# Context attention with gate and the query, key and value projections as two unrolled stages over four batches

## The reference, cut to what matters

```python
memory_proj = einsum('bme,de->bmd', memory, W_mem)             # memory: (4, 1601, 256)
scores = einsum('bnd,bmd->bnm', hidden, memory_proj) / sqrt(512)
attn = softmax(scores)
memory_context = einsum('bnm,bmd->bnd', attn, memory_proj)
gate = sigmoid(concat([hidden, memory_context]) @ W_gate.T + b_gate)
x = rmsnorm(hidden + gate * memory_context, norm_w)            # the norm of the first layer
...
vm = expert_mask(token_type_ids)                               # by token: v or l expert
y = rmsnorm(x, ln_in_w)
mixed = where(vm, y @ v_qkv, y @ l_qkv)                        # (4, 512, 1536): q, k, v
q, k = rotary(q, k)
```

## Time and profile before

| | |
|---|---|
| median of 3 runs | 2446.51 us (2446.05 to 2450.79) |
| the profiled execution | 2442.05 us, its span 2440.2 us |
| busy share of the span: PE, DVE, ACT, POOL | 86%, 63%, 40%, 19% |
| mean granted clock of TensorE | 0.912 |
| set-up | 0 to 30.0 us |
| four passes of the loop | 30.0 to 805.4 us |
| self-attention | from 805.4 us |

### The profile page before, as it was taken

How to read it: one execution, slowest core, us unless ns; L and a number is a source line. 1 busy time by engine, 2 the same in 40 slices (tenths; PEclk the granted TensorE clock), 3 DMA queues, 4 the chain that set the end, 5 groups by cost and what they waited for, 6 DMA issues and landing times. The chain is left out here.

```text
span 2440.2 us, 33165 instructions
## 1 busy us (share of the span) xinstructions
PE 2094.5 (86%) x12597; PEld 1365.8 (56%) x12614; DVE 1537.2 (63%) x2208; ACT 973.9 (40%) x1707; POOL 473.7 (19%) x483
## 2 busy tenths in 40 slices
PE   5985985986798699958883999999999799999868
PEld 3673664664566355547771344444443578778756
DVE  5176367376458477664446899999993466666444
ACT  1132132222223255525440688888888222221111
POOL 0211211211103011132220022222222122122111
PEclk8987987988898699989995899999999899999979
DMA  4026025224313866345648243445430234334232
GB/s 154 26 80 222 18 74 184 68 61 146 119 44 125 190 149 167 85 151 208 232 175 165 32 82 77 86 88 93 78 77 15 81 92 114 89 105 117 68 92 70
DMA packets 192596, 262.29 MB, mean 107 GB/s; under 512 B 27896, under 2 KB 108924, under 8 KB 190612
## 3 DMA queue, kind: packets, MB, share of 16 engines
q1 hardware_dynamic: 184278, 248.68, 37.7%
q0 software_dynamic: 7856, 10.90, 1.7%
q10 hardware_dynamic: 288, 0.27, 0.0%
HBM read 193.20 MB, written 64.47 MB: 106 GB/s over the span
## 5 line engine op out<-in xcount | busy, mean ns | idle before, releaser
L1638 DVE TENSOR_REDUCE quarters<-ps 128x2 f32<-128x804 f32 x512 | 483.1, 991 | 51.8 <-PE ps L1672 50.4
L1603 ACT ACTIVATE pT_x<-ps 128x512 f32<-128x512 f32 (+1 forms) x832 | 451.6, 595 | 104.1 <-PE ps L1700 76.7
L1672 PE MATMUL ps<-kx_ring,qx_ring 63*128 63x402 f32 x1024 | 234.0, 469 | 41.0 <-DMA kx_ring<-cross_k_by_part 29.1
L1715 PE MATMUL ps<-pT_x,vx_ring 128*17 128x256 f32 (+1 forms) x3328 | 261.5, 387 | 0.2 <-ACT osb_x L1585 0.2
L190 DVE TENSOR_TENSOR w_lo<-w_raw,w_hi 128x512 fp32r<-128x512 f32 (+3 forms) x309 | 244.7, 792 | 10.6
L188 DVE CAST w_hi<-w_raw 128x512 fp32r<-128x512 f32 (+3 forms) x309 | 157.3, 509 | 138.8 <-PE ps L196 94.0
L1672 PEld LDWEIGHTS ps<-kx_ring,qx_ring 63*128 63x128 f32 x1024 | 100.3, 193 | 233.9 <-DVE quarters L1638 123.3
L194 PE MATMUL ps<-mi_h,w_hi 128*128 128x512 f32 (+1 forms) x440 | 175.0, 398 | 37.3 <-issue 26.1
L1700 PE MATMUL ps<-qx_ring,kx_ring 64*128 64x512 f32 (+1 forms) x832 | 175.0, 417 | 6.4 <-ACT pT_x L1603 2.6
L196 PE MATMUL ps<-mi_l,w_hi 128*128 128x512 f32 (+1 forms) x440 | 174.3, 396 | 0.0
L195 PE MATMUL ps<-mi_h,w_lo 128*128 128x512 f32 (+1 forms) x440 | 173.5, 394 | 0.0
(11 more groups left out here) (271 smaller groups left out, 4450.1 us busy)
## 6 DMA issues: line engine op xcount, KB each, us to landing
kx_ring<-cross_k_by_part SPq DMA_DIRECT2D x96, 200.2 KB, 7.4
w_raw<-L_xattn_l_qkv SPq DMA_DIRECT2D x48, 256.0 KB, 2.9
w_raw<-L_xattn_v_qkv SPq DMA_DIRECT2D x48, 256.0 KB, 2.7
q_ring<-self_q_by_part SPq DMA_DIRECT2D x48, 256.0 KB, 4.1
k_ring<-self_k_by_part SPq DMA_DIRECT2D x48, 256.0 KB, 6.5
w_raw<-L_xattn_l_gate SPq DMA_DIRECT2D x40, 256.0 KB, 2.9
w_raw<-L_xattn_l_up SPq DMA_DIRECT2D x40, 256.0 KB, 2.9
w_raw<-L_xattn_l_down SPq DMA_DIRECT2D x40, 256.0 KB, 2.7
```

The source lines that it names most:

```text
L1603: nc.scalar.activation(pT[0:kn, u % 3, j, :], ps[0:kn, 5 + v % 3, :], ACT.Exp, scale=SCALE)\
L1638: nc.vector.tensor_reduce(out=quarters[:, g % 2, pair, :, q, quarter], in_=ps[:, at:at + 2, 0:MAXW], axis=AX.X, op=ALU.max)\
L1672: last = nc.tensor.matmul(ps[:, at + par, 0:MAXW], q_r[rows, g % RING, pair, q * P:(q + 1) * P], k_r[rows, g % RING, pair, k0:k0 + MAXW], ...
L1715: last = nc.tensor.matmul(ps[j * HD:j * HD + CHD + 1, 4, queries], v_r[0:kn, g % RING, kt, j, :], pT[0:kn, u % 3, j, queries], start=kt == ...
```

## The change

The set-up, the loop and its two blocks are replaced by two blocks that go over all batches, written out one batch after another.

`gated_context` does the set-up and, for each batch, the attention to the context and the gate up to `h`, which it stores as `fused_d` (not yet normed). The split memory weight, `w12`, the transposed memory weight and the x half of the gate weight stay in SBUF for all batches. x has two buffers. The loads of the next batch are issued inside the current one. Row maxima are found in halves of two banks each, alternating with `gate_from_x`, which now does one output tile at a time. The scores use two banks instead of three. The projection of the next x stands between the last steps of a batch.

`queries_values_keys` begins with the last batch (its h is still in SBUF), splits all 24 weight tiles once and keeps them, rounding them on ScalarE and subtracting on VectorE. For each batch the order is queries, values, keys (before: queries, keys, values). The four rotations of the keys are done within the first pieces of the next batch. The squares and their sums use four tiles, and the results go to memory piece by piece from small rings. The first norm's row is stored as `norm_d`, and `projections` applies it with the norm weight to the loaded stream.

```diff
+            for n in range(RAW, len(tiles)):
+                load_w(sp, n, tiles[n], wl, s["s_ws"])
+            for b in range(B):
+                if b:
+                    sp.wait_ge(s["s_g"], 2 * DT * b)
+                    sp.dma_start(fused_d[b - 1], h[:, :, :]).then_inc(s["s_up"], 16)
+                if b + 1 < B:
+                    load_x(b + 1)
+                    load_context(b + 1)
+                    load_rows(b + 1)
+            sp.wait_ge(s["s_g"], 2 * DT * B)
+            sp.dma_start(fused_d[B - 1], h[:, :, :]).then_inc(s["s_up"], 16)
+            sp.wait_ge(s["s_up"], 16 * B)
...
+            for b in range(B):
+                for kt, (k0, kn) in enumerate(KEY_TILES):
+                    n = KT * b + kt
+                    act.wait_ge(s["s_sc"], n + 1)
...
+                    nc.scalar.activation(pT[0:kn, n % 3, :], ps[0:kn, other_bank(b, 2 + kt % 2), :], ACT.Exp,
...
+                    if b + 1 < B and 4 <= kt < 4 + DT:
+                        round_x(b + 1, kt - 4)
+                for e in range(ET):
+                    act.wait_ge(s["s_tm"], ET * b + e + 1)
+                    if b:
+                        act.wait_ge(s["s_b"], DT * b)
+                    nc.scalar.activation(cn_h[:, e, :], tmp[:, e, :], ACT.Copy).then_inc(s["s_cnh"], 1)
+                if b + 1 < B:
+                    round_u(b + 1)
+                    round_context(b + 1)
+                for j in range(DT):
+                    act.wait_ge(s["s_c"], DT * b + j + 1)
+                    if b:
...
+                    else:
...
+                    nc.scalar.activation(eg[:, j, :], ps[:, gate_bank(b, j), :], ACT.Sigmoid, bias=cols[:, 4, j:j + 1])\
+                        .then_inc(s["s_eg"], 1)
...
+            pe.wait_ge(s["s_tabc"], 2 + ET)
+            for b in range(B):
+                pe.wait_ge(s["s_uh"], ET * (b + 1))
+                pe.wait_ge(s["s_th"], NB * (b + 1))
+                if b:
+                    pe.wait_ge(s["s_eg"], DT * b)
+                for j in range(DT):
+                    maxima(b, 2 * j)
+                    maxima(b, 2 * j + 1)
+                    gate_from_x(b, j)
+                pe.wait_ge(s["s_mx"], HALVES * (b + 1))
+                pe.wait_ge(s["s_dg"], ST * (b + 1))
+                scores(b, 0)
+                scores(b, 1)
+                for kt in range(KT):
+                    values(b, kt)
+                    if kt + 2 < KT:
+                        scores(b, kt + 2)
+                if b + 1 < B:
+                    project(b + 1, 0)
+                pe.wait_ge(s["s_un"], ET * (b + 1))
+                pe.wait_ge(s["s_acc"], KT * (b + 1))
+                for q in range(ST):
+                    last = nc.tensor.matmul(ps[:, other_bank(b, 0), q:q + 1], acc[:, q * P:(q + 1) * P], ones[:, 0:1],
+                                            start=True, stop=True)
+                last.then_inc(s["s_sum"], 1)
+                if b + 1 < B:
+                    project(b + 1, 1)
+                pe.wait_ge(s["s_rq"], b + 1)
+                for q in range(ST):
+                    last = nc.tensor.matmul(ps[:, other_bank(b, 1), q * P:(q + 1) * P],
+                                            rq[:, q:q + 1].broadcast_to((P, P)), ident[:, :], start=True, stop=True)
+                last.then_inc(s["s_rep"], 1)
+                if b + 1 < B:
+                    project(b + 1, 2)
+                    project(b + 1, 3)
+                for k in range(ET):
+                    pe.wait_ge(s["s_cnl"], ET * b + k + 1)
+                    for j in range(DT):
+                        cut = slice(j * P, (j + 1) * P)
+                        last = three(ps[:, gate_bank(b, j), :], w12h[:, k, cut], w12l[:, k, cut],
+                                     cn_h[:, k, :], cn_l[:, k, :], False, k == ET - 1)
+                        if k == ET - 1:
+                            last.then_inc(s["s_c"], 1)
+                if b == 0:
+                    pe.wait_ge(s["s_ws"], DT + ET)
                 for j in range(DT):
                     cut = slice(j * P, (j + 1) * P)
+                    if j == 2 and b + 1 < B:
+                        pe.wait_ge(s["s_ul"], ET * (b + 2))
+                    for k in range(ET):
+                        last = three(ps[:, other_bank(b, j), :], wth[:, k, cut], wtl[:, k, cut],
+                                     cn_h[:, k, :], cn_l[:, k, :], k == 0, k == ET - 1)
+                    last.then_inc(s["s_b"], 1)
...
+weights, GROUPS, G = [t["L1_xattn_l_qkv"], t["L1_xattn_v_qkv"]], (0, 2, 1), 2 * DT
+NT, NK = 3 * G, 6
+turns = [B - 1] + list(range(B - 1))
...
+            for i in range(B):
+                store_keep(i)
+                if i:
+                    for j in range(DT):
+                        store_piece(2 * DT * (i - 1) + DT + j)
+                if i + 1 < B:
+                    sp.wait_ge(s["s_x"], 2 * DT * (i + 1))
+                    sp.wait_ge(s["s_sq"], 2 * DT * (i + 1))
+                    sp.dma_start(h[:, :, :], fused_d[turns[i + 1]]).then_inc(s["s_hin"], 16)
+                    load_tokens(i + 1)
+                sp.wait_ge(s["s_rs"], 4 * i + 2)
+                sp.dma_start(norm_d[turns[i]:turns[i] + 1, :], rs0[0:1, :]).then_inc(s["s_r0u"], 16)
+                for j in range(DT):
+                    store_piece(2 * DT * i + j)
+                for a in range(ST):
+                    sp.wait_ge(s["s_vn"], ST * i + a + 1)
+                    sp.dma_start(vs_d[turns[i]].rearrange("g p a n -> p a g n")[:, a, :, :],
+                                 v_nat[:, a % 2, :].rearrange("p (g n) -> p g n", n=P)).then_inc(s_uv[a % 2], 16)
...
+                round_x(0, n)
+                round_w(n)
             for n in range(2):
                 for k in range(DT):
+                    square(0, n, k)
+            for n in range(G, 2 * G):
+                round_w(n)
+            for i in range(B):
+                if i:
+                    keep_plain(i - 1, 1)
+                    for j in range(2):
+                        round_piece(2 * DT * (i - 1) + DT + j)
+                root(i, 0)
+                if i:
+                    for j in range(2, DT):
+                        round_piece(2 * DT * (i - 1) + DT + j)
+                root(i, 1)
+                keep_plain(i, 0)
+                if i == 0:
+                    for n in range(2 * G, 3 * G):
+                        round_w(n)
+                for j in range(DT):
+                    round_piece(2 * DT * i + j)
+                keep_values(i)
+                if i + 1 < B:
+                    for n in range(2 * DT):
+                        round_x(i + 1, n)
+                        square(i + 1, n // DT, n % DT)
+            keep_plain(B - 1, 1)
...
+            def sums(i, n):
+                pe.wait_ge(s["s_sum"], 3 * (2 * i + n + 1))
+                if i:
+                    pe.wait_ge(s["s_t2"], 2 * DT * (i - 1) + DT + n + 1)
+                nc.tensor.matmul(ps[:, bank(3 * i + 1, n), :], ones[:, :], sq[:, 2 + n, :], start=True, stop=True)\
+                    .then_inc(s["s_ss"], 1)
+            def run(i, t0):
+                for n in range(3 * G):
+                    project(i, n, t0)
+                    if n < 2 and i:
+                        rotate(i - 1, 1, 2 * n)
+                        rotate(i - 1, 1, 2 * n + 1)
+                    if n == 3:
+                        sums(i, 0)
+                        sums(i, 1)
+                    if G <= n < G + 2:
+                        rotate(i, 0, 2 * (n - G))
+                        rotate(i, 0, 2 * (n - G) + 1)
+                    if n == G + 4:
+                        pe.wait_ge(s["s_t2"], 2 * DT * i + 1)
+                        pe.wait_ge(s["s_tab"], 5 * i + 3)
+                        for a in range(ST):
+                            last = nc.tensor.matmul(ps[:, bank(3 * i, 0), a:a + 1], rs1[0:1, a * P:(a + 1) * P], ones[0:1, 0:1],
+                                                    start=True, stop=True)
+                        last.then_inc(s["s_rc"], 1)
+            for i in range(B):
+                pe.wait_ge(s["s_k"], NK * (i + 1))
+                early = nc.tensor.value_load(early_v[0:1, turns[i]:turns[i] + 1], min_val=0, max_val=1)
+                with nc.tensor.If(early > 0):
+                    run(i, 0)
+                with nc.tensor.If(early < 1):
+                    run(i, S - P)
+            for j in range(DT):
+                rotate(B - 1, 1, j)
...
-                sp.dma_start(streams[b % 2][:, :, :], gated_d[b]).then_inc(s["s_hin"], 16)
+                sp.dma_start(streams[b % 2][:, :, :], fused_d[b]).then_inc(s["s_hin"], 16)
+                if b:
+                    sp.wait_ge(s["s_scl"], DT * b)
+                sp.dma_start(norm_rows[:, :], norm_d[b:b + 1, :].broadcast_to((P, S))).then_inc(s["s_hin"], 16)
...
-                dve.wait_ge(s["s_hin"], 16 * (b + 1))
+                dve.wait_ge(s["s_hin"], 32 * (b + 1))
+                for j in range(DT):
```

(25 more changed lines are left out.)

974 lines of the change are left out of this document (508 added, 466 removed).

## The result

The changed kernel takes 2308.91 us (median of 4 runs, 2307.88 to 2309.82), against 2447.73 us before on the same chips: ratio 0.943, 95% interval 0.9415 to 0.9448. That is 139 us less; 129 to 130 us were forecast, and the forecast time was 2316 us. The profiled execution spans 2308.0 us, against 2440.2, 132 us less.

The account below looks back on a forecast made before the run. TensorE's order of work was taken to bound a pass while it works, nothing useful at the seams. Self-attention's start moves from 805.4 to 674 us, less 2: 129 to 130 us gained, 2312 profiled, 2316 median; range 2272 to 2376.

Parts of the forecast that it names:

- set-up, to the first row maximum: Start of the kernel: constants land at 12 us, then TensorE and ScalarE work; 39 us, range 34 to 45, against 46.7 before.
- context stage: Attention to the context and gate, all batches: 79 us of TensorE work plus 0.9 us hand-overs per batch, stalls covered.
- the seam: Between the two new blocks: last VectorE steps, store, barrier, token load and small steps; TensorE starts again at 378.4 us.
- second stage, first batch: First batch of queries, values and keys: 76.7 us, with 12.9 us waiting and 128-column pieces at the lower clock.
- three more batches: Later batches of queries, values and keys, weights resident: 65.2 us each, 195.6 us together, including 7 us clock loss each.
- tail, to self-attention: After the last keys: four uncovered rotations, VectorE and ScalarE steps in turn, store and barrier; 23 us, ending at 674 us.
- the projections: Stage applying the first norm by four VectorE steps of 0.75 us per batch; only the first batch pays, 2 us.
- The wait for the sums: Second stage, first batch: TensorE stands still from 391 us until GpSimd has added ScalarE's squares, at 403 to 404; 12.9 us.
- I take half of the loss and the return, 3.5 us: Blocks of 48 narrow matmuls, second stage: half of 4.8 us clock loss, about half of 2 us return; 7 us per batch.
- Rival (a): Clock holds in the second stage's narrow blocks: 8 x 3.5 = 28 us less, 2288 us; chance 0.17.
- Rival (b): Second stage bound by the chain ScalarE, GpSimd, VectorE: sharing costs 13.4 us per batch, 54 us, 2370 us; chance 0.21.
- Adding 4.5 us to the sum: Whole kernel: the median of the runs lies 4.5 us above the profiled execution, so 2312 becomes 2316 us.

## Why the prediction was right, and where its terms were off

The sum was right to 2 us for the profiled execution (2312 forecast, 2309.8 measured), and the mechanism is shown by the experiments. But that it came within 2 us is luck, since terms that were off by up to 14 us balance each other:

| step | forecast | measured | off by |
|---|---|---|---|
| set-up, to the first row maximum | 39 | 47.1 | +8.1 |
| context stage | 321.6 | 322.2 | +0.6 |
| the seam | 17.8 | 18.4 | +0.6 |
| second stage, first batch | 76.7 | 77.8 | +1.1 |
| three more batches | 195.6 | 181.8 | -13.8 |
| tail, to self-attention | 23 | 15.8 | -7.2 |
| the projections | +2 | +9.8 | +7.8 |

- **Set-up.** Too short. The step was "I let them land at 12 us, more than twice the 5.4 us of a 1 MB load alone". They landed at 19.7 us. Beside them stood 5.2 MB of loads on the other queue, not the 4 MB of the estimate, and the small ones waited their turn among these. With these held back they landed at 12.9, which is the number that the estimate was good for.
- **Context stage.** Right: 83.3 us for the first batch and 79.3 for the next two, where 83.7 and 79.9 were said. The last took 80.3, not 78.1; by the prediction's own terms it is 79.9 - 5.6 + 4.7 = 79.0, so 78.1 left the hand-overs out. The alternation of maxima and gate (2.7 us), the projection between the last steps (10.3) and the loads a batch ahead (15.2) each showed its worth when undone.
- **Second stage, first batch.** The sum hit, the parts less. The wait for the sums was 6.9 us, not 12.9, since ScalarE began its squares 9.2 us after TensorE's start, where the prediction had VectorE's eight steps end at 12.6, and the additions took 1.26 to 1.47 us instead of 1.54. TensorE's first four pieces and the sums took 22.2 us (26.1 forecast), the narrow block 10.9 (10.2), the values 24.3 (20.3), the keys 20.3 (20.1). In the values' time are the 3.7 us for rs_col, which the prediction didn't have. Nor did it price in this batch what sets the start of the values, the root behind ScalarE's eight roundings of weights: its product ended 0.3 us before the narrow block was through, so that the wait and the half clock that it did price stood beside a chain of the same length.
- **The other three.** The step that failed was "I take half of the loss and the return, 3.5 us". The narrow block of the queries took 5.73 us at clock 1.00, where 48 x 0.214 = 10.3 us is the price at the lower level. What remains over the work of 56.7 us is 2.3 to 2.5 us ahead of each batch, where the branch stands (the profile charges them to a low part of x), and some 2 us of clock. Rival (a), with a chance of 0.17, is what happened in these three batches. Taken alone, its 28 us less would have been too much: the first batch did lose its block, and the other three kept 3 to 4 us each of pause and clock.
- **Sharing between VectorE and GpSimd.** Rival (b) did not decide. The sharing is there: from 465 us on, 16 of VectorE's masks of x took 1205 ns in the mean, against 749 before. A mask took 1.63 to 1.68 us beside an addition of GpSimd and 0.75 without one. That is 7 us of VectorE's time, and the last subtractions and the rotations add some 8 us by their means (0.77 to 0.96 us against 0.69): about 5 us per batch, not 13.4. And in these three batches TensorE waited for it for nothing longer than the 2.3 to 2.5 us at the start.
- **Tail.** 15.8 us instead of 23; the last rotations began at 647.3, the last store was issued at 659.7 and the barrier took the rest, so the steps overlap more than the estimate let them.
- **The projections.** That only the first batch pays for the multiplications was right: without them the first sum into h came 286.5 us after self-attention's first load instead of 288.3. What was missing is the lengthening of the later batches, by some 3 us each. Taking the row's load away as well gave at most 2.5 us of it; the rest goes with the clock, and its trigger is open.
- **Median and profile.** The profiled execution of before was 5 us under its median, that of the changed kernel at its median. Adding 4.5 us to the sum made the forecast of the median worse.

## What to carry to other kernels

Where an engine stands still at the seams of a loop, move the next pass's first product between the last small steps of this one, and its loads a pass ahead: undone, these cost 10 and 15 us per batch here. Keeping weights resident was worth more by the work, and the waits for loads, that it took from the engine that copies for TensorE than by TensorE's own waits for weights. Before an edit takes away a wait, follow what hangs behind it. The sums placed later gave nothing and the squares placed earlier gave 6.6 us, since only these brought forward the root that the values wait for. A block that runs at half the clock costs nothing where such a chain ends with it. And ahead of the first matmul, large loads that are needed late should wait for the small ones that are needed at once.

## What was not expected of the hardware

The same 48 matmuls of 128 columns ran at granted clock 1.00 (5.5 to 5.7 us) where TensorE had been busy ahead of them with a pause of at most 0.2 us, and at 0.50 (10.9 us) where waits of 2.2 and 4.7 us stood ahead. Narrowness alone does not bring the lower clock here; before the change such blocks had pauses within them and a mean of 0.67. In the projections a batch of the same instructions took 54.8 or 58.0 us. Ahead of the stretch that differed stood a pause of 3.39 us where the clock held and one of 3.44 us where it fell, too near to each other to be the cause alone.
